# Counting matmuls of a graph layer: groups taken two at a time, with products of sums between them

## What is computed

```python
h = layernorm(x)
msg = h[src] + relvectors[edge_type]
red = segment_sum(msg, dst)              # 200,000 edges into 6250 nodes
x = x + gru_cell(red, h)
g = layernorm(x)
idx = top_k(g @ Wg + bg, 2)              # two of 8 experts for each node
x = x + sum over the two experts of gelu(g @ W1[e] + b1[e]) @ W2[e] + b2[e]
```

## Time and profile before

| | us |
|---|---|
| median of 3 runs (lowest, highest) | 1694.0 (1689.6, 1695.6) |
| the profiled execution | 1692.4 |
| its span | 1690.5 |
| PE busy | 1397.3 (83%) |
| DVE busy | 1075.3 (64%) |
| POOL busy | 1033.4 (61%) |
| ACT busy | 708.9 (42%) |

### The profile page before, as it was taken

How to read it: one execution, slowest core, us unless ns; L and a number is a source line. 1 busy time by engine, 2 the same in 40 slices (tenths; PEclk the granted TensorE clock), 3 DMA queues, 4 the chain that set the end, 5 groups by cost and what they waited for, 6 DMA issues and landing times.

```text
span 1690.5 us, 39892 instructions
## 1 busy us (share of the span) xinstructions
PE 1397.3 (83%) x14228; PEld 1172.8 (69%) x14228; DVE 1075.3 (64%) x3958; ACT 708.9 (42%) x1538; POOL 1033.4 (61%) x948
## 2 busy tenths in 40 slices
PE   1269999999999999999888989885465999989990
PEld 1247878887877778877777778674464977777770
DVE  7767676776676786679788788954454544444440
ACT  7333334343444444434333332222133766556660
POOL 2277667677766677577777776777712444445452
PEclk8568999999999999999899898786776999999995
DMA  9676334454544444444454443448413454555446
GB/s 312 168 221 202 113 94 121 129 151 118 144 131 132 131 129 115 118 141 132 141 147 129 133 126 102 118 122 319 123 43 99 81 84 78 84 79 85 79 74 172
DMA packets 136165, 220.58 MB, mean 130 GB/s; under 512 B 27761, under 2 KB 101046, under 8 KB 134688
## 3 DMA queue, kind: packets, MB, share of 16 engines
q0 software_dynamic: 63872, 123.12, 30.3%
q1 hardware_dynamic: 72096, 94.84, 18.3%
HBM read 169.05 MB, written 57.76 MB: 134 GB/s over the span
## 4 chain that ended last, share of the span: by engine, by line
PE 38%; DMA 20%; DVE 16%; POOL 10%; issue 7%; ACT 5%; SPq 1%; DVEq 1%; POOLq 0%; ACTq 0%
DMA out_rows<-yo,xrows 13%; PE P L1573 12%; PE P L1538 11%; POOL out_rows L659 5%; PE P L1521 4%; DMA raw<-in_L_ffn_W_dram 4%; POOL ring L614 4%; PE P L1483 3%; DVE cone L1072 3%; DVE lone L1071 2%; PE P L1525 2%; DMA ring<-h_table,idx 2%; ACT amat L716 2%; PE P L1474 1%; POOL expert_rows L623 1%
## 5 line engine op out<-in xcount | busy, mean ns | idle before, releaser
L614 POOL DMA_INDIRECT ring<-h_table,idx x728 | 724.8, 996 | 341.4 <-issue 255.3
L716 ACT ACTIVATE amat<-P 128x300 f16<-128x300 f32 (+3 forms) x608 | 240.4, 428 | 618.6 <-PE P L1525 611.3
L1538 PE MATMUL P<-hs,amat 128*126 128x256 f16 (+4 forms) x2646 | 329.3, 282 | 0.0
L1538 PEld LDWEIGHTS P<-hs,amat 128*126 128x126 f16 (+4 forms) x2646 | 300.4, 139 | 4.9
L659 POOL DMA_INDIRECT out_rows<-yo,xrows x112 | 177.4, 1584 | 206.3 <-DMA out_rows<-yo,xrows 163.4
L1521 PE MATMUL P<-cone,lone 128*128 128x294 f16 (+3 forms) x840 | 217.8, 295 | 62.6 <-DVE cone L1072 44.0
L1072 DVE TENSOR_SCALAR cone<-iota,comb 128x294 f16<-128x294 f16 (+3 forms) x840 | 262.9, 316 | 0.0
L1071 DVE TENSOR_SCALAR lone<-iota,slo 128x128 f16<-128x128 f16 x840 | 222.8, 266 | 2.9 <-PE P L1521 2.4
L623 POOL DMA_INDIRECT expert_rows<-xrow,slots x100 | 122.3, 1223 | 70.4 <-DVE slots L1201 40.8
L1751 PE MATMUL P<-xh,w_all 128*128 128x256 f16 x896 | 157.8, 274 | 7.6 <-issue 7.6
L1764 PE MATMUL P<-w_all,gh 128*128 x896 | 149.8, 273 | 0.7 <-DVE gl L1412 0.6
(11 more groups left out here) (230 smaller groups left out, 2676.2 us busy)
## 6 DMA issues: line engine op xcount, KB each, us to landing
raw<-in_L_ffn_W_dram SPq DMA_DIRECT2D x32, 512.0 KB
xrows<-expert_rows SPq DMA_DIRECT2D x56, 257.0 KB, 2.7
ring<-h_table,idx POOLq DMA_INDIRECT x728
w_parts<-parts SPq DMA_DIRECT2D x16, 512.0 KB
w_all<-w_parts SPq DMA_DIRECT2D x8, 1024.0 KB
h_in<-h_table SPq DMA_DIRECT2D x25, 250.0 KB
x<-in_x_dram SPq DMA_DIRECT2D x25, 250.0 KB
out_rows<-x SPq DMA_DIRECT2D x25, 250.0 KB
```

The costliest lines, as they stand in the source:

```text
L614: nc.gpsimd.indirect_dma_start(out=ring[:, r, j, :], out_offset=None, in_=h_dram, in_offset=bass.IndirectOffsetOnAxis(ap=idx[:, slot, g * ...
L716: nc.scalar.activation(amat[:, b % 2, :, s * aw:(s + 1) * aw], P[2 + g % 2][:, 0:HIS * aw].rearrange("p (h w) -> p h w", w=aw), ACT.Copy). ...
L1538: nc.tensor.matmul(to, amat[:, b % 2, hi, 0:used], hs[:, hi, part * D:(part + 1) * D], start=(hi == 0 and part == 0), stop=False)
```

## The change

PE takes the groups of a half-step in bursts: two groups of one or two chunks make a burst, a group of four chunks or a last odd one is a burst of its own (`bursts_of`). `head_burst` waits once at its head, for the last chunk of the burst (`a_ready`), for the copy of the group two before the last of the burst (`a_moved`), and for `a_windows` where it has risen; then it issues the wide matmuls of both groups and behind them the narrow ones of both. The first burst stands where the first half of the groups stood. The piece of the half-step is cut into as many parts as there are bursts, and the parts stand between and behind the later bursts. ACT copies the groups of the first burst where it copied the first half. DVE's order is as it was.

Of 250 bursts of two, 29 are in h = 0 to 16, 168 in h = 17 to 100 and 53 in h = 101 to 144. In the first 101 half-steps the first burst holds the same two groups as the first half (or, with three groups, one more). From 101 to 144 a half-step with three groups had one group in its first half and now has two in its first burst, and DVE still builds the second of these after its stages.

The general path now takes its sums in the order of the tiles: for each band it runs over windows of the runs of neighbouring tiles (`band_runs`, `band_column`).

```diff
+def bursts_of(h):
+    out = []
+    for g in groups_of(h):
+        if out and len(out[-1]) == 1 and GROUPED[g][2] < GC and GROUPED[out[-1][0]][2] < GC:
+            out[-1].append(g)
+        else:
+            out.append([g])
+    return out
...
@@ ACT, fast path
-                    mine = groups_of(h)
-                    for g in mine[:len(mine) // 2]:
+                    bursts = bursts_of(h)
+                    for g in bursts[0] if bursts else []:
                         move_group(g)
...
-                    for g in mine[len(mine) // 2:]:
+                    for g in groups_of(h)[len(bursts[0]):] if bursts else []:
                         move_group(g)
...
@@ PE
-            def head_group(g):
-                row, c, k, aw = GROUPED[g]
-                pair = HEAD // 2 - 1 - row // 2
-                at = GC * (row % 2) + c
-                to = P[2 + g % 2]
-                if g >= 2:
-                    pe.wait_ge(a_moved, g - 1)
-                for n in range(k):
-                    seq = SC * pair + SC - at - k + n
-                    pe.wait_ge(a_ready, seq + 1)
-                    nc.tensor.matmul(to[:, 0:HI * aw], lone[:, seq % BUFS, :], cone[:, seq % BUFS, 0:HI * aw],
-                                     start=(n == 0), stop=(n == k - 1)).then_inc(a_used, 1)
-                pe.wait_ge(a_windows, pair + 1)
-                for n in range(k):
-                    ins = nc.tensor.matmul(to[0:R, HI * aw:HIS * aw], tone[:, pair % 2, at + n, :],
-                                           wone[:, pair % 2, at + n, 0:aw], start=(n == 0), stop=(n == k - 1))
-                ins.then_inc(a_group, 1)
+            def head_burst(groups):
+                if groups[-1] >= 2:
+                    pe.wait_ge(a_moved, groups[-1] - 1)
+                pair, at, k, aw, seq = chunk_of(groups[-1])
+                if pair + 1 > seen[0]:
+                    seen[0] = pair + 1
+                    pe.wait_ge(a_windows, pair + 1)
+                pe.wait_ge(a_ready, seq + k)
+                for g in groups:
+                    pair, at, k, aw, seq = chunk_of(g)
+                    for n in range(k):
+                        nc.tensor.matmul(P[2 + g % 2][:, 0:HI * aw], lone[:, (seq + n) % BUFS, :], cone[:, (seq + n) % BUFS, 0:HI * aw],
+                                         start=(n == 0), stop=(n == k - 1)).then_inc(a_used, 1)
+                for g in groups:
+                    pair, at, k, aw, seq = chunk_of(g)
+                    for n in range(k):
+                        ins = nc.tensor.matmul(P[2 + g % 2][0:R, HI * aw:HIS * aw], tone[:, pair % 2, at + n, :],
+                                               wone[:, pair % 2, at + n, 0:aw], start=(n == 0), stop=(n == k - 1))
+                    ins.then_inc(a_group, 1)
...
-            def head_piece(b, n, pieces):
+            def head_piece(b, n, pieces, m, of):
...
-                for hi in range(HI * n // pieces, HI * (n + 1) // pieces):
+                for hi in range(HI * (n * of + m) // (pieces * of), HI * (n * of + m + 1) // (pieces * of)):
...
@@ PE, fast path
-                    for g in mine[:len(mine) // 2]:
-                        head_group(g)
+                    if bursts:
+                        head_burst(bursts[0])
...
-                    if h in PIECE_AT:
-                        head_piece(*PIECE_AT[h])
-                    for i in stage_of(h, 10):
-                        rank(i)
-                    for g in mine[len(mine) // 2:]:
-                        head_group(g)
+                    of = max(len(bursts), 1)
+                    for m in range(of):
+                        if h in PIECE_AT:
+                            head_piece(*PIECE_AT[h], m, of)
+                        if m == 0:
+                            for i in stage_of(h, 10):
+                                rank(i)
+                        if m + 1 < len(bursts):
+                            head_burst(bursts[m + 1])
```

95 lines of the change are left out of this document (66 added, 29 removed).

## The result

| | before | after |
|---|---|---|
| median of 16 runs, us (lowest, highest) | 1693.5 (1688.7, 1700.6) | 1707.6 (1696.2, 1715.1) |
| the profiled execution, us | 1692.4 | 1709.4 |
| its span, us | 1690.5 | 1707.6 |

One of the 16 runs after took 1994.3 us at a granted clock of 0.63 and is left out of the range and the ratio (without it the median is 1706.6 us). The ratio is 1.0076, 95% interval 1.0053 to 1.0099: some 13 us slower, where 1671 us was forecast and the range ended at 1694. The page of the changed kernel shows TensorE less busy (1397.3 us before) and waiting longer: L1587 is the wide matmul now, L1592 the narrow one, L1605 and L1609 the piece, L1548 the counts, L1531 and L1540 the sums; its group stands against the wide one of the earlier trace rows.

What follows compares the result with a forecast made beforehand. PE was taken to bound the one-chunk half-steps, PE and DVE in turns the two-chunk ones, with POOL close behind. Terms -28.6 - 4 + 3 + 7 - 2.5 + 2.5 = -22.6 gave 1671 us, range 1648 to 1694.

Steps and rivals of the forecast that it cites:

- switches, h 17-100: One-chunk half-steps: 168 bursts each save 0.17 us of wide-narrow switches on PE, -28.6 us.
- waits for ACT there: h 17 to 100: piece parts behind bursts cover ACT's copies, -7, half-steps without a piece +3, together -4 us.
- waits for DVE there: h 17 to 100: later bursts come earlier and uncover DVE's building of chunks, 14 tiles x 0.5, +7 us.
- ring: From 367 to 447 us POOL has only 3 us of slack to follow a faster PE, +3 us.
- clock: Whole kernel: fewer slow stretches in one-chunk half-steps, perhaps more in two-chunk ones; 0 taken for the pair.
- h 17-100 in all: One-chunk half-steps: terms for switches, ACT's copies, ring and DVE, -28.6 - 4 + 3 + 7 us.
- h 0-16: First half-steps, led by first gathers and DVE: half of 29 x 0.17 us saved, -2.5 us.
- h 101-144: Two-chunk half-steps: switches save 4.5 us, lateness from waiting at the burst's head costs 7, together +2.5 us.
- h 145-159: These half-steps and later: single bursts, nothing changes, 0 us, between -2 and +3.
- Rivals 1 and 4: Switches: 1, waits are the cost or clock rises, 1650 us, chance 0.14; 4, no switches saved, 1698 us, 0.08.
- the general path: Code of the general path: not executed in this run, so its edits cost nothing, 0 us.
- rival 3: Two-chunk half-steps: waits at the burst's head for late second groups, 42.6 us, all paid; 1702 us, chance 0.09.

Runs made afterwards that it cites:

- e4: Kernel before, order and waits untouched, narrow matmul's weights widened from 16 to 128 columns; ratio 0.9884 to the kernel before.
- e1: Changed kernel's bursts and split pieces only in half-steps whose groups all have one chunk (h 0 to 100), the others as before; ratio 0.9959 to the kernel before.
- e2: Changed kernel's bursts, head waits and split pieces only in h 101 to 159, the others as before; ratio 1.0093 to the kernel before.
- e14: Changed kernel with the second group of h 101 to 144 in its old place and each group and chunk waiting for itself; ratio 0.9940 to the kernel before.
- e13: Changed kernel, waits still gathered, but the second group of h 101 to 144 in its old place; ratio 0.9997 to the kernel before.
- e7: Changed kernel with the piece whole ahead of the second burst instead of split; ratio 1.0104 to the kernel before.
- e5: Changed kernel's order, but each group waits for its own bank and each wide matmul for its own chunk; ratio 1.0012 to the kernel before.
- e3: Kernel before with only the piece split between and behind the later groups; single groups with their own waits; ratio 0.9954 to the kernel before.
- e12: e4 plus two 128-column matmuls behind each group whose results nobody reads; ratio 0.9958 to the kernel before.
- e6: Changed kernel with DVE building all groups of the first burst in its first half; ratio 1.0062 to the kernel before.
- e8: Kernel before with e3's split piece and e4's widened narrow matmul together; 1663.5 us, ratio 0.9817 to the kernel before.
- e9: e8 with the relation counts and the product of L1542 also padded to 128 columns or rows; 1664.7 us, ratio 0.9836 to the kernel before.
- e10: Changed kernel with e5's fine waits and e6's order of DVE together; ratio 1.0014 to the kernel before.

## Why the prediction was wrong

Its sum was -22.6 us and the spans differ by +17.1. Stretch by stretch:

| step of the prediction | forecast | measured |
|---|---|---|
| switches, h 17-100 | -28.6 | 168 x 0.174 = -29.2 by the pitches |
| waits for ACT there | -4 | +8.2 |
| waits for DVE there | +7 | +6.1 |
| ring | +3 | +1.3 |
| clock | 0 | +3.5 |
| h 17-100 in all | -22.6 | -6.4 (the rows above add to -10; of the 4 left, 3 lie in PE's busy time and are not explained) |
| h 0-16 | -2.5 | +1.0 |
| h 101-144 | +2.5 | +17.0 |
| h 145-159 | 0 | +2.9 |
| behind, experts, ahead | 0 | +2.6 |

**What held.** The price of a switch, and that the shape and not the wait is what costs: the pitches after are the forecast's to 0.01 us, and e4 removes the price with all waits in place. Rivals 1 and 4 fall with it. DVE's catching-up (+6.1 for +7), the ring (POOL waits 48.3 us for PE in half-steps 17 to 100, had 57.7), the general path (its code is in e1, e2 and e14 too, which are faster or slower for other reasons; by itself it wasn't run).

**What failed first: h 101 to 144, +2.5 for +17.** The step was "I find it kept at the turn from DVE's lead to PE's, once for each of 7 tiles": it had the mechanism, and rival 3's 42.6 us of late groups, and took a sixth of it, 7 us. Measured, PE's idle time there grew by 21.5 us, half of the 42.6, and the stretch by 17.0. The reason given, that lateness behind a leading DVE is free, is true behind the gates (e13: 18 us more waiting there, nothing lost) and false ahead of them (after: 20 us more there, 17 lost). The prediction looked at who leads, not at what stands behind the waiting instruction. It also left the clock out: 0.93 fell to 0.90, by the clock records 41.0 to 58.0 us at 1.2 GHz, half of which, 8.5 us, is in the 17. e13 and e14, with the group in its old place, have 37.5.

**What failed second: ACT's waits, -4 for +8.2.** That "a part of the piece stands behind each burst and covers the copies" holds (without it, in e7, PE waits 16 us more for ACT), but a gathered wait asks for the copy of the burst's second group at its first. Half-step 31 shows another part of it, on the timeline of PE:

```profile
264.34 0.30 PE L1587 MATMUL P<-cone,lone 128*128 128x294 f16 x1 [1.76 <-ACT amat L758]
```

and on that of ACT:

```profile
262.01 0.83 ACT L785 ACTIVATE rT<-P,half_rz 128x250 f32<-128x250 f32 x2
262.73 1.14 ACT L814 ACTIVATE parts<-raw,scales 128x1024 f16<-128x1024 f32 x1
263.77 0.22 ACT L748 ACTIVATE cts<-P 16x96 f16<-16x96 f32 x1
263.90 0.70 ACT L758 ACTIVATE amat<-P 128x300 f16<-128x300 f32 x2
```

The third burst waits for the copy of the first group of the second, and that copy stands in ACT's list behind 1.9 us of a gate and a weight conversion. Such fifth groups of a half-step have 13.4 of the 23.7 us that groups wait for ACT there; but they had 10.8 of 15.4 before, so they are only 2.6 of the growth. Second bursts are 5.0 of it (1.4 to 6.4 us). Split as the prediction's term was: in half-steps with a piece it took 7 us off, and the waits rose by 2.7 (12.7 to 15.4); in those without it added 3, and they rose by 5.5 (2.7 to 8.2). With fine waits (e5) they come to 19.0 in all, so gathering is more than half of the +8.2. The earlier trace rows gave the duration of a copy; what the copy stands behind in ACT's list was never looked at.

**The clock, 0 for +3.5 there and +8.5 in the next stretch.** The prediction set two effects of opposite sign against each other and took none. Runs with bursts spend 44 to 61 us of half-steps 17 to 100 at 1.2 GHz, those without bursts and with single narrow groups (before, e2, e3) 34 to 38, at idle times of 35 to 54 and 24 to 26 us. The +3.5 is from the lowest of them; e1 and e13, the same code there, make it +12 and +10, so this term is worth 3 to 12 us. Idle time alone doesn't set it: e12 idles 36.2 us and has 17.1 us at 1.2 GHz. The page TensorE: Matmul & The Clock Gate of the Trainium skill (HAM oscillation), which the prediction named, says that idle gaps between bursts of matmuls bring back the slow clock. It had the sign right in both stretches (idle time and time at 1.2 GHz both rose); the size came from runs alone.

**h 0 to 16, -2.5 for +1.0.** PE is busy 5.6 us less there, for 29 bursts, and idles 6.6 more (13.4 to 20.0). Neither the gain nor a loss can be told: before and e2, with the same order there, took 90.0 and 93.5 us.

**h 145 to 159, 0 for +2.9.** Its bursts are single groups, so nothing seemed to change; but a group of four chunks now waits for its fourth ahead of its first. With fine waits (e5) the stretch is 93.8 us, as before (93.7).

**Not explained:** the experts, 469.1 us against 464.2. e6, nearest to the change, has 468.5, all others between 460.3 and 464.6. Nothing in their code differs.

By ratios, the change can be laid out along a path of runs: the split piece -0.46% (e3), bursts with fine waits in their old place another -0.14% (e14 against e3, within the intervals of both), gathered waits +0.6%, the new place of the second group +0.75%. That they sum to the measured +0.76% is no proof of its own, as each step is a difference of two runs on the way; the steps that stand clear of noise are the first and the last two.

## What to carry to other kernels

Before gathering waits or moving work forward in one engine's list, write down what stands behind the instruction that will wait, and who waits for that: 31 us of waiting, 23 of them behind the gates, cost nothing, and 39 us, 32 of them ahead of the gates, went with a stretch 17 us longer. If a change of shape is the price, change the shape (here 16 to 128 weight columns, 1.2% faster) rather than the order, which brings waits of its own; and where other engines follow PE closely (here it was busy 95% of the stretch), expect much of what it saves to come back as its own idle time: 56 to 73% in half-steps 17 to 100 of after, e4, e8 and e9.

## What the runs showed of the hardware

- A matmul with 16 weight columns behind one with 128 starts 0.09 us later than one of 128 columns would (0.217 to 0.219 against 0.125), and the way back costs 0.07 (0.105 against 0.030). It isn't the direction: behind a matmul of 6 columns the step from 128 to 16 weight columns costs 0.07 too (e4, narrow to counts: 0.097), and behind the counts, of 48 columns, the step from 16 to 126 costs 0.09 (0.113; 0.025 in e9, where both are full). Weights of 16 rows among those of 128 (L1542) cost 0.09 on either side (0.203 and 0.200 against 0.109). Weights of 125 or 126 columns (`amat`) beside 128 cost nothing. The Trainium skill, TensorEngine Tiling, Key Properties, states that a change of mode drains the engine and one of tile doesn't; the trace agrees if 16 and 126 columns are taken as two modes and 126 and 128 as one, and padding undoes it.
- A wait that is already satisfied costs no more than 0.01 us: wide to wide of 294 columns within a burst is 0.125 us without a wait between (after) and 0.126 with one or two (e10).
- More matmuls can cost less than their work: 67 us of them cost 12.5 us of the kernel (e12), as in half-steps 17 to 100 the clock rose from 0.95 to 0.98 and idle time fell.
